# Output projection of a two-FFN transformer block: where its first loads stand, how many PSUM banks a chunk takes, and where its last six chunks stand

## The chip, the cores and the metric

The kernel runs on one core of a Trainium2 chip. A core has five engines with a queue of their own, each in order: TensorE (PE), VectorE (DVE), ScalarE (ACT), GpSimd (POOL) and SyncE (SP), which here only issues DMAs. They meet at semaphores. The metric is the device time of one execution in microseconds (us), as the median of several runs.

## The reference

The input x has 8 sequences of 1024 rows of 256 numbers, 8192 rows in all. Three residual steps follow each other:

```python
x = x + 0.5 * ffn(layernorm(x))     # gate/up 256 -> 704, SiLU, down 704 -> 256, every operand quantized to FP4 by blocks of 16
x = x + attn(layernorm(x))          # 16 heads of 16, causal softmax, then out @ Wo.T
x = x + 0.5 * ffn(layernorm(x))
```

The piece that matters here is the last product of the attention, `out @ Wo.T`, added to x, and the first rows of the second feed-forward.

## The kernel before, in words

The whole x stays in SBUF as `xs` (64 tiles of 128 rows). Four blocks follow each other, each ended by a barrier of all engines: feed-forward 0, the q/k/v projection, attention, and a last block in which the output projection stands ahead of feed-forward 1 (`feed_forward(1, store=True, begin=...)`). Within a block the order on each engine is the order in which its code is written; nothing is scheduled.

Attention works through 32 groups (8 sequences of 4 groups of 4 heads). A group's result is not yet divided by the softmax sums. SP carries it there: `send_half` writes the two halves (`o_all`) and their sums (`sum_rows`) to DRAM, `load_sums` brings the sums back and repacks the rows (`o_rows`), DVE takes the reciprocal (`one_over`), `load_group` sends it out (`inverse_rows`), spreads it over rows (`inverse_all`), and loads group and inverse, POOL multiplies (`divide`), and `send_out` stores into `attn_cols`, which holds the attention's output transposed, 256 x 8192. For the last group, the steps from `load_sums` on stand in the last block, among the output projection's own.

The output projection goes by 16 chunks of 512 rows. For chunk c: SP loads 256 x 512 numbers (512 KB) from `attn_cols` into one of four buffers (`out_a`, semaphore `a_loaded`); ACT rounds them to a high part (`out_aT_hi`), DVE takes the rest as the low part (`out_aT_lo`), both with two buffers; PE makes 24 matmuls (4 tiles of 128 rows, 2 halves of the contraction, 3 products of high and low parts) into two banks of PSUM; DVE adds the banks to `xs` (semaphore `resid`). A step of DVE is: low part of chunk c+1, then the sum of chunk c. PE's chunk c waits for `out_aT_lo` of c and for the sum of c-2; ACT's high part of c+1 waits for its load and for PE's chunk c-1.

`begin[name](eng, part)` stands ahead of the feed-forward's steps i = -6, -5 and -4 (`steps`). Part 0 holds chunks 0 to 11, part 1 chunks 12 and 13, part 2 chunks 14 and 15. Those feed-forward steps fill its pipeline: at step i DVE takes the layernorm's sums of tile i+6, ACT makes z of tile i+5 from POOL's `shift`, DVE reduces and quantizes z of tiles i+4 and i+3, PE transposes tile i+1 (`xT`), and the gate and up products of tile i come at step i (from step 0). In step i, DVE's `ffn_amax` of z leads to POOL's `ffn_dscale`, POOL's `ffn_shift` stands behind that, and ACT's next `ffn_z` waits for it.

Of the kernel before, what the change touches and what calls it, by code (L numbers as in the profile page):

```python
# [13 lines left out]
P = 128  # L14
# [12 lines left out]
CHUNK = 512  # L27
# [40 lines left out]
def build(nc, x_in, wq_in, wk_in, wv_in, wo_in, wg_in, wu_in, wd_in, y_out):  # L68
    V, S, G, T = nc.vector, nc.scalar, nc.gpsimd, nc.tensor
    top = ExitStack()  # L70
    with top:
# [41 lines left out]
        ring = [group_buffers(top, 0)]  # L113

# [222 lines left out]
        A_RING = 4  # L337
        a_loaded = [sem(f"a_loaded{i}") for i in range(A_RING)]

        def output_projection(ctx, last_group):  # L340

            s = out_sem
            CT = CHUNK // P
            CHUNKS = ROWS // CHUNK
            attn_in = sb(ctx, "out_a", [P, A_RING, KD, CHUNK], F32)
# [3 lines left out]
            def done(eng, name, c):  # L352
                if isinstance(c, int) and c < 0:
                    return
                eng.wait_ge(s[name], c + 1)

            def has(c):
                return not isinstance(c, int) or 0 <= c < CHUNKS

            def chunks(eng, step, part):  # L360

                if part == 0:
                    for c in range(-1, A_RING):
                        step(c, c % A_RING, c // A_RING)
                    with eng.Fori(1, CHUNKS // A_RING - 1) as turn:
                        for n in range(A_RING):
                            step(turn * A_RING + n, n, turn)
                for c in ((), (CHUNKS - 4, CHUNKS - 3), (CHUNKS - 2, CHUNKS - 1))[part]:
                    step(c, c % A_RING, c // A_RING)

            load_sums, load_group, send_out = last_group["sync"]

            def sync(sp, part):
                def step(c, r, turn):
                    if has(c):
                        done(sp, "aT_lo", c - A_RING)
                        sp.dma_start(attn_in[:, r, :, :], attn_cols[:, bass.ds(c * CHUNK, CHUNK)]
                                     .rearrange("(k p) c -> p k c", p=P)).then_inc(a_loaded[r], 16)
                    if isinstance(c, int) and c == A_RING - 1:
                        load_group(sp)  # L380

                if part == 0:
                    load_sums(sp)
                if part == 2:
                    send_out(sp)
                    sp.wait_ge(ao_stored, 32 * BATCH * GROUPS)
                chunks(sp, step, part)

            def tensor(pe, part):
                def step(c, r, turn):  # L390
                    if has(c):
                        done(pe, "resid", c - 2)
                        done(pe, "aT_lo", c)
                        for t in range(CT):
                            for k in range(KD):
                                for n, (x, w) in enumerate(passes(aT, woT)):
                                    last = T.matmul(proj_ps[r % 2][t // 2][:, (t % 2) * DIM:(t % 2 + 1) * DIM],  # L397
                                                    x[:, r % 2, k, t * P:(t + 1) * P], w[:, k, :],
                                                    start=k == 0 and n == 0, stop=k == KD - 1 and n == 2)
                        last.then_inc(s["proj"], 1)  # L400

                chunks(pe, step, part)
                if part == 2:
                    done(pe, "resid", CHUNKS - 1)

            def scalar(act, part):
                def step(c, r, turn):
                    if has(c + 1):
                        buf = (r + 1) % 2
                        nr, nturn = (r + 1) % A_RING, turn + (r + 1) // A_RING  # L410
                        act.wait_ge(a_loaded[nr], nturn * 16 + 16)
                        done(act, "proj", c - 1)
# [4 lines left out]
                chunks(act, step, part)  # L417
# [5 lines left out]
            def vector(dve, part):  # L423
                def step(c, r, turn):
                    if has(c + 1):
                        buf = (r + 1) % 2
                        done(dve, "aT_hi", c + 1)
                        for k in range(KD):
                            last = V.tensor_tensor(aT[1][:, buf, k, :], attn_in[:, (r + 1) % A_RING, k, :],  # L429
                                                   aT[0][:, buf, k, :].bitcast(F32), ALU.subtract)  # L430
                        last.then_inc(s["aT_lo"], 1)
                    if has(c):
                        done(dve, "proj", c)
                        for u in range(2):
                            rows = xs[:, bass.ds(c * CT + 2 * u, 2), :].rearrange("p t c -> p (t c)")
                            last = V.tensor_tensor(rows, proj_ps[r % 2][u][:, :], rows, ALU.add)  # L436
# [1157 lines left out]
```

## Time and profile before

| | |
|---|---|
| median of 3 runs | 2201.95 us (2199.97 to 2202.27) |
| profiled execution | 2202.19 us |
| its span in the trace | 2200.2 us, so 2.0 us lie around the span |
| attention's last value products on PE | until about 1660 |
| output projection on PE | 1671 to 1730 |
| first gate product of feed-forward 1 | 1740.46 |
| then to the end | about 6.8 us a tile |

The times in the trace are microseconds from the span's start. In the rows, a figure in brackets is the idle time of the engine ahead of an instruction, and what ended it. `SPq` is the queue of SP. PEclk is the granted clock of TensorE, 1.00 for 2.4 GHz and 0.50 for 1.2 GHz. A time for PE is one of pipelined matmuls, so neighbours overlap. An "x2" or "x24" is a run of like instructions merged into one row.

### The profile page before, as it was taken

To read this page: it belongs to the slowest core of one execution; us is meant where nothing else is said; L and a number is where in the kernel's file an instruction comes from. 1 tells how busy PE (TensorE), PEld (TensorE's weight loads), DVE (VectorE), ACT (ScalarE), POOL (GpSimd) and SP (SyncE) were. 2 spreads that over 40 slices of the span, in tenths; PEclk is the share of its full clock that TensorE was granted. 3 is DMA by queue.
4 is the path that set the end of the run, shared out by engine and by line. 5 is a ranking of instruction groups with operands and counts; after the bars stand their busy time and mean duration, and the time that the engine had idled before them with its cause. 6 is when DMAs were issued, how large, how long until landed. Compare 5 with 4: busy or idle time off the path is not lost. (4 is left out here: it accounts for less than half of the span.)

```text
span 2200.2 us, 44394 instructions
## 1 busy us (share of the span) xinstructions
PE 2041.9 (93%) x13448; PEld 1335.3 (61%) x13448; DVE 1906.2 (87%) x4327; ACT 1287.6 (59%) x2221; POOL 1037.8 (47%) x1639
## 2 busy tenths in 40 slices
PE   4799999997999799999999999999996799999998
PEld 3688888886885233333333333333335688888887
DVE  6799999996987789898888888898853699999996
ACT  3455555542763477777777777777783345555553
POOL 4788888883655011111111111111110388888884
PEclk9899999997997799999999999999998999999998
DMA  6000000001689477777777777877624100000000
GB/s 213 1 1 0 0 0 0 0 0 38 226 237 208 54 120 138 133 128 132 131 131 131 123 131 133 137 124 134 120 79 155 48 15 19 19 19 19 19 20 25
DMA packets 163502, 184.91 MB, mean 84 GB/s; under 512 B 57696, under 2 KB 109280, under 8 KB 163040
## 3 DMA queue, kind: packets, MB, share of 16 engines
q1 hardware_dynamic: 160672, 182.11, 39.6%
q8 instruction: 71, 1.16, 0.2%
q10 hardware_dynamic: 2688, 1.05, 0.2%
q14 instruction: 71, 0.58, 0.1%
HBM read 113.90 MB, written 85.98 MB: 91 GB/s over the span
## 5 line engine op out<-in xcount | busy, mean ns | idle before, releaser
L1476 POOL TENSOR_SCALAR_AFFINE_SELECT diag_scores<-diag_scores 128x256 f32<-128x256 f32 (+1 forms) x192 | 94.5, 493 | 581.4 <-ACT diag_scores L1439 577.5
L1512 DVE CUSTOM_DVE_ANT_0 gu_ps<-gu_ps,mask_qk 128x256 f32<-128x256 f32 x511 | 291.7, 597 | 73.7 <-PE gu_ps L1299 71.7
L1441 ACT ACTIVATE probs<-hT_ps 128x512 f32<-128x512 f32 (+3 forms) x320 | 273.7, 855 | 133.4 <-PE hT_ps L1321 75.9
L1299 PE MATMUL gu_ps<-k_stack,q_stack 96*128 96x512 bf16 (+3 forms) x994 | 319.2, 349 | 21.0 <-DVE part_max L1512 8.6
L721 PE MATMUL gu_ps<-wguT_hi,ffn_xT_hi 128*128 128x512 f32 (+1 forms) x768 | 313.1, 408 | 7.3 <-DVE ffn_xT_lo L597 5.1
L1340 PE MATMUL gu_ps<-probs,v_group 128*17 128x512 f32 (+3 forms) x3072 | 312.5, 494 | 2.2 <-ACT probs L1441 1.1
L721 PE MATMUL gu_ps<-wguT_hi,ffn_xT_lo 128*128 128x512 f32 (+1 forms) x768 | 290.2, 378 | 0.0
L721 PE MATMUL gu_ps<-wguT_lo,ffn_xT_hi 128*128 128x512 f32 (+1 forms) x768 | 289.8, 377 | 0.0
L699 ACT ACTIVATE ffn_z<-xs,ffn_shift,ffn_rstd 128x256 f32 (+1 forms) x128 | 77.1, 602 | 349.5 <-POOL ffn_shift L650 349.5
L1441 ACT ACTIVATE probs<-av_ps 128x512 f32<-128x512 f32 (+3 forms) x320 | 275.3, 860 | 0.6 <-PE av_ps L1321 0.5
L1299 PEld LDWEIGHTS gu_ps<-k_stack,q_stack 96*128 96x128 bf16 x994 | 91.8, 98 | 294.6 <-DVE part_max L1512 157.7
L1316 PE MATMUL hT_ps<-q_stack,k_stack 98*128 98x512 bf16 (+3 forms) x768 | 230.4, 330 | 8.6 <-DMA q_stack<-max_rows 8.2
L1517 DVE TENSOR_REDUCE part_max<-gu_ps 128x1 f32<-128x512 f32 x351 | 227.3, 678 | 10.3 <-PE gu_ps L1299 8.2
L620 POOL TENSOR_TENSOR ffn_hq<-ffn_g_h,ffn_nscale 128x704 f32<-128x704 f32 (+1 forms) x256 | 210.5, 843 | 3.5 <-DVE ffn_g_h L584 3.5
L752 PE MATMUL xd_ps<-wdT_hi,ffn_hT_hi 128*128 128x256 f32 x640 | 193.0, 302 | 20.5 <-DVE ffn_hT_lo L536 20.5
L1316 PE MATMUL av_ps<-q_stack,k_stack 98*128 98x512 bf16 (+3 forms) x768 | 193.4, 326 | 1.6 <-ACT probs L1441 1.3
L669 POOL TENSOR_TENSOR ffn_v_h<-ffn_h,ffn_rec 128x704 f32<-128x704 f32 x128 | 178.2, 1392 | 16.9 <-DVE ffn_rec L580 7.3
L752 PE MATMUL xd_ps<-wdT_lo,ffn_hT_hi 128*128 128x256 f32 x640 | 183.2, 286 | 0.0
L752 PE MATMUL xd_ps<-wdT_hi,ffn_hT_lo 128*128 128x256 f32 x640 | 183.2, 286 | 0.0
L1195 POOL TENSOR_TENSOR o_group<-o_group,o_inverse 128x512 f32<-128x512 f32 x32 | 40.7, 1272 | 267.4 <-DMA o_inverse<-inverse_all 267.4
L721 PEld LDWEIGHTS gu_ps<-wguT_hi,ffn_xT_hi 128*128 128x128 f32 x768 | 146.3, 191 | 26.8 <-DVE ffn_xT_lo L597 7.4
L721 PEld LDWEIGHTS gu_ps<-wguT_hi,ffn_xT_lo 128*128 128x128 f32 x768 | 145.5, 189 | 23.4
(211 smaller groups left out, 5120.0 us busy)
## 6 DMA issues: line engine op xcount, KB each, us to landing
q_stack<-q_parts SPq DMA_DIRECT2D x192, 128.0 KB, 7.0
k_stack<-k_parts SPq DMA_DIRECT2D x192, 128.0 KB, 7.6
o_all<-o_sb SPq DMA_DIRECT2D x64, 256.0 KB
q_parts<-qkv_parts SPq DMA_DIRECT2D x32, 384.0 KB, 2.7
k_parts<-qkv_parts SPq DMA_DIRECT2D x32, 384.0 KB, 2.8
v_ones<-qkv_vst SPq DMA_DIRECT2D x16, 544.0 KB, 3.8
v_group<-v_ones SPq DMA_DIRECT2D x32, 272.0 KB, 11.0
xs<-in_L_attn_x SPq DMA_DIRECT2D x8, 1024.0 KB, 12.0
```

Source lines behind the costliest of these rows:

```text
L620: last = G.tensor_tensor(blocks(hq[:, to:to + n]), blocks(g_h[:, of:of + n]), spread(nscale[:, par, of // BLK:(of + n) // BLK]), ALU.mult)
L669: G.tensor_tensor(blocks(v_h[:, par, :]), blocks(h[:]), spread(rec[:, OF_H]), ALU.mult).then_inc(s["v_h"], 1)
L699: S.activation(z[:, 1 - par, :], x_tile(i + 5), ACT.Identity, bias=shift[:], scale=rstd[:]).then_inc(s["z"], 1)
L721: last = T.matmul(gu_ps[:, n, 0:cols.stop - cols.start], x[:, buf, k * P:(k + 1) * P], w[:, k, cols], start=k == 0 and m == 0, stop=k == K ...
L752: T.matmul(down_ps, x[:, k * P:(k + 1) * P], w[:, k, :], start=k == 0 and n == 0, stop=False)
L1299: mm = T.matmul(out[:, e, :], qs[0:STACK, h0 + e, t * P:(t + 1) * P], ks[0:STACK, h0 + e, c * CHUNK:c * CHUNK + w], start=True, stop=True)
L1316: mm = T.matmul(scores[pair][:, e, at:at + w], ks[0:STACK_MAX, h, t * P:(t + 1) * P], qs[0:STACK_MAX, h, (j + 1) * CHUNK - w:(j + 1) * CHUNK],
L1340: mm = T.matmul(o_ps[h * VPAD:h * VPAD + VCOLS, CHUNK - w:CHUNK], vs[:, t, h, :], probs[:, h // 2, i % 2, h % 2, at:at + w], start=first, ...
L1441: S.activation(probs[:, pair, i % 2, :, first:w], scores[pair][:, :, first:w], ACT.Exp, scale=DH ** -0.5).then_inc(s[pr], 1)
L1476: G.affine_select(out=block_of, in_=block_of, compare_op=ALU.is_ge, fill=MASKED, base=0, pattern=[[0, 2], [0, count], [1, P]], channel_mul ...
L1512: last = V.tensor_tensor_reduce(out=ps[:, e * w:(e + 1) * w], in0=ps[:, e * w:(e + 1) * w], in1=mask_qk[:, CHUNK - w:CHUNK], scale=1.0, sc ...
L1517: last = V.tensor_reduce(part_max[:, h0:h0 + per, t, c], ps[:, 0:per * w].rearrange("p (h w) -> p h w", h=per), AX.X, ALU.max)
```

## The change

1. The buffers `out_a` are gone. The four chunk buffers are now the memory of the first group's `q_stack0` and `k_stack0` (two chunks each), which the last sequence's last three groups no longer use.
2. The loads of chunks 0 to 3 are issued by SP in the attention block, at its end: behind the last group's `load_inverse` (of the group before), ahead of its `send_half`.
3. `load_group` is cut in four steps, and in the last block they stand between loads: load 4, `send_inverse`, load 5, `spread_inverse`, load 6, `load_group`, load 7, `load_inverse`, load 8, 9, `send_out`, then the others.
4. A chunk's PSUM is `gu_ps` banks 0 and 1 for even chunks and the two banks of `hT_ps` for odd ones (before: `gu_ps` 0 and 1, `gu_ps` 2 and `xd_ps`). So ACT's copy, DVE's subtraction and DVE's sum are one instruction of 1024 columns a chunk each, where they were two of 512.
5. Part 0 holds chunks 0 to 9, and parts 1 to 6 one chunk each (10 to 15), ahead of the feed-forward's steps -5 to 0. `one_over` of the last group stands behind DVE's step 1 instead of step 0. All of it is unrolled, where chunks 4 to 11 were a loop.

```diff
+        attn_in = [ring[0][r // 2][:, :, :].bitcast(F32).rearrange("p h t -> p (h t)")[:, r % 2 * KD * CHUNK:(r % 2 + 1) * KD * CHUNK]
+                   .rearrange("p (k c) -> p k c", k=KD) for r in range(4)]
...
+        OUT_FIRST = 10
+        OUT_PARTS = OUT_CHUNKS - OUT_FIRST + 3
+        def load_out(sp, c):
+            out_done(sp, "aT_lo", c - A_RING)
+            sp.dma_start(attn_in[c % A_RING], attn_cols[:, c * CHUNK:(c + 1) * CHUNK]
+                         .rearrange("(k p) c -> p k c", p=P)).then_inc(a_loaded[c % A_RING], 16)
...
-            proj_ps = (bank[0:2], bank[2:4])
+            proj_ps = (gu_ps[:, 0:2, :], hT_ps[:, :, :])
+            def chunks(part):
                 if part == 0:
+                    return range(-1, OUT_FIRST)
+                return (OUT_FIRST - 1 + part,)
+
+            def sync(sp):
+                then = {A_RING: send_inverse, A_RING + 1: spread_inverse, A_RING + 2: load_group,
+                        A_RING + 3: load_inverse, A_RING + 5: send_out}
+                load_sums(sp)
+                for c in range(A_RING, OUT_CHUNKS):
+                    if c == SEQ // CHUNK * (BATCH - 1):
+                        sp.wait_ge(ao_stored, 32 * BATCH * GROUPS)
+                    load_out(sp, c)
+                    if c in then:
+                        then[c](sp)
...
+                if part == OUT_PARTS - 3:
+                    out_done(pe, "resid", OUT_CHUNKS - 2)
+                if part == OUT_PARTS - 1:
+                    out_done(pe, "resid", OUT_CHUNKS - 1)
...
-                        for k in range(KD):
-                            last = S.copy(aT[0][:, buf, k, :], attn_in[:, nr, k, :])
-                        last.then_inc(s["aT_hi"], 1)
+                        S.copy(aT[0][:, (c + 1) % 2, :, :], attn_in[(c + 1) % A_RING]).then_inc(s["aT_hi"], 1)
...
-                        if name in begin and i + AHEAD < 3:
+                        if name in begin and i + AHEAD < OUT_PARTS:
...
                         groups(sp, group)
+                        once(sp, "pv", (NG - GROUPS + 1) * NS, 0)
+                        for c in range(A_RING):
+                            load_out(sp, c)
                         send_half(*LAST, 1)
                         send_out(sp, *before(*LAST))
```

SP's queue at the seam of the two blocks, before. The names are a DMA's target and source; `out_a` are the chunk buffers.

```order
L1179 DMA o_inverse<-inverse_all 128x512 [waits att_inverse_spread]
L1239 DMA o_all<-o_sb 128x512 [waits att_o_sb]
L1240 DMA sum_rows<-o_sb 4x512
L1188 DMA attn_cols<-o_group 64x512 [waits att_ao]
L1188 DMA attn_cols<-o_group 64x512
L1232 UNCONDITIONAL_BRANCH
L770 UNCONDITIONAL_BRANCH [waits barrier_Pool_Activation_PE_DVE_SP_release]
L1159 DMA sums<-sum_rows 128x32 [waits att_inverse,att_o_sent]
L1161 DMA o_rows<-o_all 8x8192
L377 DMA out_a<-attn_cols 128x2x512 x4
L1168 DMA inverse_rows<-inverse 128x32 [waits att_inverse]
L1171 DMA inverse_all<-inverse_rows 128x1x512 [waits att_inverse_sent]
```

And with the change, from the first four loads on and from the new block's start on (the chunk buffers now read as `q_stack` and `k_stack`).

```order
L352 DMA q_stack<-attn_cols 128x2x512 [waits att_pv]
L352 DMA q_stack<-attn_cols 128x2x512
L352 DMA k_stack<-attn_cols 128x2x512 x2
L1229 DMA o_all<-o_sb 128x512 [waits att_o_sb]
```

```order
L1139 DMA o_rows<-o_all 8x8192
L352 DMA q_stack<-attn_cols 128x2x512 [waits out_aT_lo]
L1146 DMA inverse_rows<-inverse 128x32 [waits att_inverse]
L352 DMA q_stack<-attn_cols 128x2x512 [waits out_aT_lo]
L1153 DMA inverse_all<-inverse_rows 128x1x512 [waits att_inverse_sent]
L352 DMA k_stack<-attn_cols 128x2x512 [waits out_aT_lo]
L1162 DMA o_group<-o_rows 128x512 [waits att_o_packed,ao_stored]
L352 DMA k_stack<-attn_cols 128x2x512 [waits out_aT_lo]
L1169 DMA o_inverse<-inverse_all 128x512 [waits att_inverse_spread]
```

The first four loads moved ahead of the barrier and of `o_all`; loads 5 to 8 now stand each behind one of the steps that wait for the last group's inverse, where before all of them stood behind all those steps.

ACT's queue where the projection meets the feed-forward, before: the last two copies into `out_aT_hi` (two instructions each), and z, `av_ps` and `xT_hi` of the first tiles.

```order
L414 CAST out_aT_hi<-out_a 128x512 [waits out_proj,a_loaded2]
L414 CAST out_aT_hi<-out_a 128x512
L699 ACTIVATE ffn_z<-xs,ffn_shift,ffn_rstd 128x256 [waits ffn_shift,ffn_v_z]
L414 CAST out_aT_hi<-out_a 128x512 [waits out_proj,a_loaded3]
L414 CAST out_aT_hi<-out_a 128x512
L699 ACTIVATE ffn_z<-xs,ffn_shift,ffn_rstd 128x256 [waits ffn_shift,ffn_v_z]
L693 ACTIVATE av_ps<-ffn_v_z 128x256 [waits ffn_v_z,ffn_g_z,ffn_g_h]
```

With the change, chunks 11 to 15:

```order
L402 CAST out_aT_hi<-k_stack 128x1024 [waits out_proj,a_loaded3]
L678 ACTIVATE ffn_z<-xs,ffn_shift,ffn_rstd 128x256 [waits ffn_shift,ffn_v_z]
L402 CAST out_aT_hi<-q_stack 128x1024 [waits out_proj,a_loaded0]
L678 ACTIVATE ffn_z<-xs,ffn_shift,ffn_rstd 128x256 [waits ffn_shift,ffn_v_z]
L402 CAST out_aT_hi<-q_stack 128x1024 [waits out_proj,a_loaded1]
L672 ACTIVATE av_ps<-ffn_v_z 128x256 [waits ffn_v_z,ffn_g_z,ffn_g_h]
L678 ACTIVATE ffn_z<-xs,ffn_shift,ffn_rstd 128x256 [waits ffn_shift,ffn_v_z]
L402 CAST out_aT_hi<-k_stack 128x1024 [waits out_proj,a_loaded2]
L672 ACTIVATE av_ps<-ffn_v_z 128x256 [waits ffn_v_z,ffn_g_z,ffn_g_h]
L678 ACTIVATE ffn_z<-xs,ffn_shift,ffn_rstd 128x256 [waits ffn_shift,ffn_v_z]
L684 CAST ffn_xT_hi<-xd_ps 128x256 [waits ffn_xT,ffn_up]
L402 CAST out_aT_hi<-k_stack 128x1024 [waits out_proj,a_loaded3]
```

Each of the copies for chunks 12 to 15 now stands behind an `ffn_z` that waits for POOL's `ffn_shift`, and the last behind `ffn_xT_hi`, which waits for a transpose that PE makes behind chunk 14.

## Rows read from the trace of the kernel before

**Rows 1.** The page's head.
```profile
span 2200.2 us, 44394 instructions
```
**Rows 2.** Chain that ended last, in time: start, us, what.
```profile
1664.40 4.51 DMA out_a<-attn_cols
1668.94 1.15 ACT out_aT_hi L414 x2
...
1671.46 5.31 PE gu_ps L397 x24
...
1678.37 1.41 DMA inverse_rows<-inverse
1679.80 3.66 DMA inverse_all<-inverse_rows
...
1684.17 4.66 DMA out_a<-attn_cols
```
**Rows 3.** Timeline of SP's queue at the seam: start, us, engine, what.
```profile
1657.18 0.32 SPq L1179 DMA_DIRECT2D o_inverse<-inverse_all  x1
...
1661.45 1.16 SPq L1188 DMA_DIRECT2D attn_cols<-o_group  x2
1663.31 0.32 SPq L1159 DMA_DIRECT2D sums<-sum_rows  x1
...
1664.40 2.07 SPq L377 DMA_DIRECT2D out_a<-attn_cols  x4
```
**Rows 4.** Timeline of PE: chunk 4's first matmul, and one near the kernel's end.
```profile
1691.37 0.58 PE L397 MATMUL gu_ps<-woT_hi,out_aT_hi 128*128 128x256 f32 x1 [5.86 <-DVE out_aT_lo L429]
```
```profile
2181.00 0.36 PE L752 MATMUL xd_ps<-wdT_hi,ffn_hT_hi 128*128 128x256 f32 x1 [2.46 <-DVE ffn_hT_lo L536]
```
**Rows 5.** Stretches: us, busy PE, PEld, DVE, ACT, POOL, PEclk, DMA share, GB/s.
```profile
1662.70:1671.40 8.70, 0.00 (x0) 0.00 (x0) 1.29 (x2) 1.94 (x4) 0.00 (x0) 0.50 0.82 253
1740.40:1744.60 4.20, 4.14 (x11) 3.26 (x12) 1.89 (x8) 0.97 (x2) 3.02 (x8) 0.50 0.01 2
```
```profile
1671.40:1676.40 5.00, 4.94 (x23) 4.94 (x24) 1.30 (x3) 0.33 (x1) 0.00 (x0) 0.50 0.22 85
...
1691.30:1696.70 5.40, 5.33 (x25) 5.33 (x26) 2.41 (x5) 0.12 (x1) 0.00 (x0) 0.50 0.77 229
...
1711.40:1717.20 5.80, 5.80 (x49) 5.71 (x49) 4.98 (x8) 2.25 (x4) 0.00 (x0) 1.00 0.65 218
```
```profile
2181.00:2183.00 2.00, 2.00 (x11) 2.00 (x12) 0.89 (x1) 0.66 (x1) 1.38 (x2) 0.64 0.03 8
```
**Rows 6.** The same chain as in rows 2, from chunk 10's start to the feed-forward.
```profile
1711.33 4.39 PE gu_ps L397 x36
...
1718.61 0.44 DVE ffn_stats L540
...
1731.75 0.41 DVE ffn_amax L550
...
1733.06 0.61 ACT ffn_z L699
...
1739.50 0.36 ACT ffn_xT_hi L705
...
1740.46 2.93 PE gu_ps L721 x6
1743.39 0.43 PE xd_ps L737 x2
```
**Rows 7.** Timelines of DVE and POOL around the feed-forward's first step.
```profile
1719.17 1.26 DVE L429 TENSOR_TENSOR out_aT_lo<-out_a,out_aT_hi 128x512 fp32r<-128x512 f32 x2
1720.35 1.28 DVE L436 TENSOR_TENSOR xs<-gu_ps,xs 128x512 f32<-128x512 f32 x2
```
```profile
1719.33 0.55 POOL L632 TENSOR_TENSOR ffn_eps_var<-ffn_aggr,eps_tile 128x1 f32<-128x1 f32 x1 [31.66 <-DVE ffn_aggr L600]
...
1721.03 0.26 POOL L650 TENSOR_SCALAR ffn_shift<-ffn_aggr,ffn_rstd 128x1 f32<-128x1 f32 x1 [0.19 <-POOL ffn_rstd L635]
```

More of the change, by code:

```diff
@@ L346, in output_projection @@
             CT = CHUNK // P
-            CHUNKS = ROWS // CHUNK
-            attn_in = sb(ctx, "out_a", [P, A_RING, KD, CHUNK], F32)
             aT = [sb(ctx, f"out_aT_{part}", [P, 2, KD, CHUNK], F32R) for part in ("hi", "lo")]
-            proj_ps = (bank[0:2], bank[2:4])
[L352 to L358, printed above, removed]
@@ L360, in chunks @@
-            def chunks(eng, step, part):
-                if part == 0:
[L363 to L387, printed above, removed]
+            proj_ps = (gu_ps[:, 0:2, :], hT_ps[:, :, :])
@@ new lines, in output_projection @@
+            load_sums, send_inverse, spread_inverse, load_group, load_inverse, send_out = last_group["sync"]
+            def chunks(part):
+                if part == 0:
+                    return range(-1, OUT_FIRST)
[10 more added lines that the diff above has]
+                        then[c](sp)
@@ L389, in tensor @@
             def tensor(pe, part):
[L390 to L393, printed above, removed]
+                for c in chunks(part):
+                    if 0 <= c < OUT_CHUNKS:
+                        out_done(pe, "resid", c - 2)
+                        out_done(pe, "aT_lo", c)
                         for t in range(CT):
@@ L423, in vector @@
             def vector(dve, part):
[L424 to L436, printed above, removed]
-                        last.then_inc(s["resid"], 1)
-                    if isinstance(c, int) and c == 0:
+                for c in chunks(part):
+                    if c + 1 < OUT_CHUNKS:
+                        out_done(dve, "aT_hi", c + 1)
+                        V.tensor_tensor(aT[1][:, (c + 1) % 2, :, :], attn_in[(c + 1) % A_RING],
+                                        aT[0][:, (c + 1) % 2, :, :].bitcast(F32), ALU.subtract).then_inc(s["aT_lo"], 1)
+                    if 0 <= c < OUT_CHUNKS:
+                        out_done(dve, "proj", c)
+                        rows = xs[:, c * CT:(c + 1) * CT, :].rearrange("p t c -> p (t c)")
+                        V.tensor_tensor(rows, proj_ps[c % 2].rearrange("p a c -> p (a c)"), rows,
+                                        ALU.add).then_inc(s["resid"], 1)
+                    if c == 1:
                         last_group["vector"](dve)
-                chunks(dve, step, part)
-                done(dve, "resid", CHUNKS - 5 + 2 * part)
+                out_done(dve, "resid", 2 if part < OUT_PARTS - 1 else OUT_CHUNKS - 1)
             return {"sync": sync, "tensor": tensor, "scalar": scalar, "vector": vector, "gpsimd": gpsimd}
@@ L771, in _ @@
                         def _(sp):
-                            for part in range(3):
-                                if "sync" in begin:
-                                    begin["sync"](sp, part)
+                            if "sync" in begin:
+                                begin["sync"](sp)
                             with sp.Fori(0, TILES // 2) as it:
@@ L1162, in load_sums, with send_inverse @@
                              [:, 0:DH, :]).then_inc(s["o_packed"], 16)
-            def load_group(sp, b, g):
+            def send_inverse(sp, b, g):
                 n = b * GROUPS + g
@@ L1559, in _ @@
                         groups(dve, group)
-            return {"sync": (lambda sp: load_sums(sp, *LAST), lambda sp: load_group(sp, *LAST),
-                             lambda sp: send_out(sp, *LAST)),
+            return {"sync": [lambda sp, step=step: step(sp, *LAST) for step in
+                             (load_sums, send_inverse, spread_inverse, load_group, load_inverse, send_out)],
                     "vector": lambda dve: one_over(dve, *LAST), "gpsimd": lambda pool: divide(pool, *LAST)}
```

31 lines of the change are left out of this document (19 added, 12 removed).

## The prediction

> **What bounds the kernel now.** I read the page first, then the chain that ended last in order of time, then the timelines of SP, PE, DVE and POOL around the seam between attention and the last block, and last the table of stretches for TensorE's granted clock. The span is 2200.2 us [rows 1]. In the feed-forward the chain lies on PE tile after tile, so whatever lets the first gate product start sooner ends the kernel sooner by as much. That product starts at 1740.46 [rows 6]. The reader should look for what keeps it from starting earlier, and finds four things.
>
> First, the block's start. SP issues its last DMA of the attention block at 1661.45 for 1.16 us, and its first of the next block at 1663.31 [rows 3]: the barrier opens at about 1663.3. The first load of a chunk goes out at 1664.40 and takes 4.51 us; ACT's copy starts at 1668.94 and PE at 1671.46 [rows 2].
>
> Second, a hole behind chunk 3. The last group's inverse is sent at 1678.37, spread at 1679.80 in 3.66 us, and only then, at 1684.17, does SP issue load 4, which takes 4.66 us [rows 2]. PE is idle for 5.86 us ahead of 1691.37 [rows 4].
>
> Third, the clock. It is at 0.50 from 1662.7 on while PE idles, and stays there for chunk 0; it is there again for 5.40 us from 1691.3 (25 matmuls) and for 4.20 us from 1740.4 [rows 5]. At full clock 49 matmuls take 5.80 us [rows 5], so a chunk of 24 takes 2.85 us and two in a row have a pitch of about 2.9.
>
> Fourth, the seam with the feed-forward. From chunk 10's start at 1711.33 to the gate product 29.1 us pass [rows 6], for six chunks that need 17.4 at their pitch. The rest is a pipeline that fills through DVE, POOL and ACT with PE all but idle.
>
> **The change part by part.**
>
> Loads 0 to 3 in the attention block. SP is free at 1657.5, and four issues take 2.07 us [rows 3], so they are out by 1659.6, ahead of the wait for `o_sb` that held SP before. At 4.51 us [rows 2] the first lands at about 1662.1, before the barrier opens. From 1663.3, copy, low part and PE take what they took between 1668.94 and 1671.46, 2.5 us [rows 2]: PE starts at 1665.8 instead of 1671.46. Gain 5.65 us. Chunk 0 still runs at low clock, since PE idles here as well; I count no difference. Behind the four loads (2 MB) stand the last `o_all` and `sum_rows`, and `load_sums` waits for them. The first four loads kept the DMA engines busy until about 8 us after their first issue (DMA share 0.82 in the stretch to 1671.4 [rows 5]), so I put this wait's end near 1667, and load 4 at 1668.5, landing at 1673. ACT needs it when chunk 2 ends, at 1676.8: nothing, with 3.5 us to spare.
>
> Loads 4 to 8. Load 4 stands ahead of the inverse now, so the hole goes: 5.86 us, and the low clock behind it, 25 matmuls in 5.40 instead of 2.96, 2.4 us. Gain 8.3. What is late next is load 5. It stands behind `send_inverse`, which waits for `one_over`, now behind DVE's sum of chunk 1. Chunk 1 ends at about 1673.9 (5.2 at low clock, 2.9), its sum takes 1.28 [rows 7], so the inverse is there at 1675.5, load 5 goes out at 1675.9 and lands at 1680.6; ACT would take it at the end of chunk 3, 1679.7. Load 6 waits for the inverse's 1.41 us [rows 2] and shares the engines with the spread of 3.66 us: out at about 1678, landing near 1684, needed at 1683.5. Loads 7 and 8 come in time by the same count, by 1 to 2 us. I take 1.5 us for these waits; the bounds are 0 (all in time) and 5.9 (the old hole).
>
> Chunks 0 to 9 together: chunk 9 ends 12.4 us sooner than at 1711.33, at about 1698.9.
>
> Chunks 10 to 15 among the feed-forward's steps. Every engine keeps its order, so I follow the loop. From chunk 9's end: the sum of chunk 9 takes 1.28 [rows 7], the layernorm's statistics until POOL starts 0.72 (1718.61 to 1719.33 [rows 6, 7]), the low part of chunk 11 1.26 [rows 7]: PE starts chunk 11 at 3.3 instead of 2.9. POOL needs from 1719.33 to 1721.29 for its first three instructions [rows 7], `ffn_z` 0.61 [rows 6], then come the copy of chunk 12, 1.15 [rows 2], and its low part: 2.0 + 1.96 + 0.61 + 1.15 + 1.26 = 7.0. From here on one turn of the loop is: sum 1.28, statistics 0.44, from `ffn_amax` to the end of `ffn_z` 1.92 (1731.75 to 1733.67 [rows 6]), copy 1.15, low part 1.26, in all 6.05 us. Two turns bring chunk 14 to 19.1. PE takes 2.85 for it, then transposes, 0.43, ACT's `xT_hi` 0.36 [rows 6], the copy and low part of chunk 15, 2.4, and chunk 15, 2.85: 28.0, and with six handovers of 0.1 28.6. The gate product then follows at once, against 29.1 before. Gain 0.5: each turn costs the projection 3 us that it did not wait before, and hides as much of the filling.
>
> The cover is thin here. PE has 2.85 us of work in 6.05, so nothing on PE hides a slow turn; a tenth of a microsecond in the loop counts three times.
>
> The gate product at full clock. It comes straight behind chunk 15, not behind 7 us of near idleness. The 4.20 us at 0.50 [rows 5] go: gain 2.1.
>
> The clock in the new gaps. PE now idles for about 3.2 us ahead of chunks 13, 14 and 15. Rows 4 and 5 show that a gap of 2.46 us near the kernel's end was enough: the clock was at 0.64 over the 2 us behind it. A chunk at low clock takes 5.2 instead of 2.85. For chunk 13 this is hidden (it may end 2.9 us late), for 14 and 15 it is 2.35 each on the path. The bounds are 0 and 4.7, or 6.8 with the gate product; I take 1.5, since a slow chunk 13 fills its own gap.
>
> The Trainium skill says in "TensorE: Matmul & The Clock Gate", section "Loop structure matters more than you think", that matmuls spread out between long waits run cold, however the waits come about. It speaks against spreading the chunks; by it alone both chunks and the gate product would be slow, the term 6.8 and the time 5.3 us above mine.
>
> One instruction for two. Two neighbours of 512 columns take 1.26 to 1.28 us on DVE [rows 7]; one of 1024 does the same columns, and I count no gain. The extremes are nothing and one start, some 0.1 us, on each of the three instructions in a turn, 1 us in all; a loss I exclude, the same elements being read and written. The last load and the output's stores are far from any wait.
> The Trainium skill's "VectorE: DVE Perf Modes", section on the TRN2 errata, gives an f32 `tensor_tensor` of N columns (N+151)/0.96 ns, so 1.22 us for 1024, an estimate from that page. It would put 0.05 us per DVE pair on my sum's good side, some 0.4 us over the path.
>
> Sum: -5.65 - 8.3 + 1.5 - 0.5 - 2.1 + 1.5 = -13.5 us against this execution's 2202.19, so 2188.7 us. The median of the runs shown, 2201.95, stands 0.24 below the profiled one; I say 2188.5 us.
>
> **The rivals.**
>
> A. SP's order makes a new hole. For it: loads 5 to 8 each stand behind a step that waits for the same inverse as before, and my margins are 1 us or below. If every step slips by one landing under load (4.66 instead of the 3 or so left), the old 5.86 comes back nearly whole with its slow clock: 5.9 + 2.4 - 1.5 = 6.8 us worse, 2195.3. Against it: the inverse is asked for 3 us sooner, and one load is ahead of it.
>
> B. The clock falls in every gap, including the one before the gate product. 5.3 us worse, 2194. For it: rows 4 and 5 at the end of the kernel. Against it: chunk 15 leads straight into the gate product.
>
> C. All goes better: no wait at loads 5 and 6, no fall of the clock, and the single instructions save 1 us. 4 us better, 2184.5.
>
> D. Slower than before. The low clock takes hold at chunk 12 and lasts through the filling of the feed-forward, since that has gaps as well. Its price: 4.7 for chunks 14 and 15, 2.1 for the first tile, and 2.5 us for each further tile whose PE work is on the path; it decides from about four tiles on, 4.7 + 2.1 + 10 - 1.5 = 15.3, time 2204. Against it: the low stretches with dense work in rows 5 ended within 5.4 us of it.
>
> E. The early loads do not help: the barrier's opening or the last group's sums move out by as much, or PE's end of attention does not matter. At 5.65 us lost and load 4 late by some 5 more, 2199. Against it: they are issued before SP's wait for `o_sb` ends.
>
> **How the numbers follow.** My forecast, 2186 to 2191, gets 0.55; A 0.12; B 0.12; C 0.14; E 0.04; D 0.02; the 0.01 left is for something unseen on the same side as D. The range leaves out D, E and the outer halves of A and C: 2184.0 to 2194.5. A measurement of this kernel tells about 0.2% from no change, 4.4 us. Faster means below 2197.5: all but D, E and the rest, 0.94. Within 0.2%: E, with a part of D, 0.04. Slower: 0.02.
>
> **What would show it.** PE's first projection matmul 2.5 us behind the barrier and no DMA ahead of ACT's first copy shows the first step. No gap over 1.5 us ahead of chunk 4, and the largest ahead of chunk 5 or 6, released through a load, shows the second. Low parts of chunks 13, 14, 15 about 6 us apart, with ACT's copies released by `ffn_z` or `ffn_shift` and PE idle for 3 us, shows the loop. The gate product's first bank in 1.4 rather than 2.93 us shows the clock term. I am wrong if chunk 9 ends less than 10 us sooner, if the turns take over 7 us, or if the feed-forward takes longer from its first gate product on than before.

## The result, and the profile after

| | before | changed |
|---|---|---|
| median of 6 runs | 2199.44 us (2198.25 to 2202.27) | 2182.62 us (2178.45 to 2185.84) |
| profiled execution | 2202.19 us | 2184.42 us |

The ratio is 0.9921, 95% interval 0.9908 to 0.9934: 16.8 us between the medians, 17.8 between the profiled executions, where 13.5 were forecast. The time is below the stated range of 2184.0 to 2194.5. Part of that is the other kernel: the range was reckoned from a median before of 2201.95, and three more runs of that kernel brought it to 2199.44. As a gain the range is 7.5 to 18.0 us, and both measured gains lie in it, near its upper end.

The page's head, after [rows 1]:

```profile
span 2182.6 us, 44275 instructions
```

The chain that ended last, after: start, us, what [rows 2, 6].

```profile
1663.53 1.05 ACT out_aT_hi L402
...
1664.61 1.24 DVE out_aT_lo L412
...
1665.89 4.51 PE gu_ps L388 x24
...
1674.40 0.35 DVE inverse L1193
...
1674.77 1.41 DMA inverse_rows<-inverse
...
1676.92 5.69 DMA k_stack<-attn_cols
...
1682.63 1.06 ACT out_aT_hi L402
...
1720.81 4.35 PE hT_ps L388 x24
1725.16 1.39 PE gu_ps L700 x6
```

No load stands ahead of the first copy. PE starts 5.57 us sooner than at 1671.46, and the gate product (its first matmul is at 1724.99 in PE's timeline) 15.5 sooner than at 1740.46. Its first bank takes 1.39 us instead of 2.93.

The timeline of SP's queue at the seam, after [rows 3]:

```profile
1656.30 1.49 SPq L352 DMA_DIRECT2D q_stack<-attn_cols  x2
1657.83 1.32 SPq L352 DMA_DIRECT2D k_stack<-attn_cols  x2
1660.65 0.33 SPq L1229 DMA_DIRECT2D o_all<-o_sb  x1
...
1667.44 0.33 SPq L1137 DMA_DIRECT2D sums<-sum_rows  x1
...
1668.53 0.44 SPq L352 DMA_DIRECT2D q_stack<-attn_cols  x1
1674.77 0.33 SPq L1146 DMA_DIRECT2D inverse_rows<-inverse  x1
```

`load_sums` comes at 1667.44 (forecast near 1667), load 4 at 1668.53 (1668.5), the inverse at 1674.77 (1675.5).

PE's timeline, after [rows 4]: chunks 6, 13, 14, 15, and the first transposes of `h`.

```profile
1685.09 0.36 PE L388 MATMUL gu_ps<-woT_hi,out_aT_hi 128*128 128x256 f32 x1 [0.40 <-DVE out_aT_lo L412]
...
1709.22 0.35 PE L388 MATMUL hT_ps<-woT_hi,out_aT_hi 128*128 128x256 f32 x1 [2.43 <-DVE out_aT_lo L412]
1714.71 0.35 PE L388 MATMUL gu_ps<-woT_hi,out_aT_hi 128*128 128x256 f32 x1 [0.90 <-DVE out_aT_lo L412]
1720.81 0.55 PE L388 MATMUL hT_ps<-woT_hi,out_aT_hi 128*128 128x256 f32 x1 [2.81 <-DVE out_aT_lo L412]
...
1744.39 0.87 PE L742 MATMUL hT_ps<-ident,ffn_hq 128*128 128x128 f32 x3 [4.39 <-POOL ffn_hq L599]
```

The hole of 5.86 us ahead of chunk 4 is gone. The 0.40 ahead of chunk 6 is the largest gap on PE until chunk 12. The other gaps are those of the loop.

Stretches, after: us, busy PE, PEld, DVE, ACT, POOL, PEclk, DMA share, GB/s [rows 5].

```profile
1665.80:1670.40 4.60, 4.51 (x26) 4.51 (x27) 1.17 (x2) 0.00 (x0) 0.00 (x0) 0.65 0.55 178
...
1709.20:1712.10 2.90, 2.88 (x16) 2.90 (x17) 2.61 (x7) 0.33 (x1) 0.88 (x3) 0.64 0.02 6
...
1720.80:1725.10 4.30, 4.29 (x25) 4.30 (x26) 2.51 (x6) 0.60 (x1) 1.72 (x5) 0.67 0.00 0
1725.10:1728.20 3.10, 3.10 (x17) 2.52 (x16) 0.84 (x3) 0.37 (x1) 0.81 (x2) 1.00 0.00 0
```

The clock is low in a part of chunks 0, 13 and 15, and whole in the gate product.

DVE's timeline, after: the low parts of chunks 12, 13 and 14, whose distance is the turn of the loop, and one sum (answers to [rows 7]).

```profile
1702.36 1.22 DVE L412 TENSOR_TENSOR out_aT_lo<-q_stack,out_aT_hi 128x1024 fp32r<-128x1024 f32 x1 [1.08 <-ACT out_aT_hi L402]
1703.50 1.22 DVE L417 TENSOR_TENSOR xs<-hT_ps,xs 128x1024 f32<-128x1024 f32 x1
...
1707.85 1.23 DVE L412 TENSOR_TENSOR out_aT_lo<-q_stack,out_aT_hi 128x1024 fp32r<-128x1024 f32 x1 [1.38 <-ACT out_aT_hi L402]
...
1713.34 1.23 DVE L412 TENSOR_TENSOR out_aT_lo<-k_stack,out_aT_hi 128x1024 fp32r<-128x1024 f32 x1 [1.37 <-ACT out_aT_hi L402]
```

A turn is 5.49 us, not 6.05. ACT's timeline in one turn, after:

```profile
1706.28 0.60 ACT L678 ACTIVATE ffn_z<-xs,ffn_shift,ffn_rstd 128x256 f32<-128x256 f32 x1 [3.96 <-POOL ffn_shift L629]
1706.79 1.03 ACT L402 CAST out_aT_hi<-q_stack 128x1024 fp32r<-128x1024 f32 x1
```

ACT stands idle for 3.96 us ahead of `ffn_z`, which waits for POOL, and the copy, which waits for nothing else, comes behind it. The copy starts 0.51 us after a z of 0.60 us, as DVE's sum starts 1.14 after a low part of 1.22: neighbours overlap by 0.08 to 0.09 us.

### The profile page after: what moved, and what is told of

Its sections match the earlier page's. It is cut to its first block and busy times, and to the rows that moved or that the text cites. A ratio compares the mean times of both kernels' runs of the same rounds, so it can differ in the third digit from the quotient of the medians.

```text
span 2182.6 us, 44275 instructions
## 1 busy us (share of the span) xinstructions
PE 2033.3 (93%) x13448; PEld 1329.3 (61%) x13448; DVE 1904.7 (87%) x4295; ACT 1285.7 (59%) x2205; POOL 1039.5 (48%) x1639
```

## The experiments

The end of attention on PE differs between executions: its last value product ends at 1659.98 in the changed kernel's trace, at 1660.95 in a second trace of the same kernel (e8), and between 1655.5 and 1661.5 in all. So I compare traces from there. "PE" is the first projection matmul, "h" the first transposes of `ffn_hq` (1744.39 above). From "h" to the span's end it is 438.3 us before and 438.2 after (436.7 to 440.0 in the experiments). The next column starts at chunk 10's first matmul, so the front of the block is left out of it. Each trace is of one execution.

| | end of attention | to PE | to h | chunk 10 to h | median, us | ratio to before, 95% |
|---|---|---|---|---|---|---|
| before | 1659.83 | 11.63 | 102.04 | 50.70 | | |
| the change | 1659.98 | 5.91 | 84.41 | 47.92 | 2182.62 | 0.9921 [0.9908, 0.9934] |
| e1_late_loads | 1656.66 | 11.45 | 93.88 | 49.35 | 2191.63 | 0.9956 [0.9939, 0.9972] |
| e2_inverse_first | 1655.59 | 5.81 | 90.04 | 46.58 | 2184.95 | 0.9942 [0.9921, 0.9962] |
| e3_no_spread | 1657.19 | 5.81 | 86.41 | 49.34 | 2184.68 | 0.9935 [0.9913, 0.9957] |
| e4_halves | 1655.55 | 6.00 | 86.95 | 48.68 | 2186.00 | 0.9940 [0.9920, 0.9960] |
| e5_copy_ahead | 1660.42 | 5.88 | 80.26 | 43.29 | 2180.12 | 0.9899 [0.9882, 0.9917] |
| e6_warm | 1656.89 | 5.81 | 84.34 | 46.59 | 2183.39 | 0.9925 [0.9907, 0.9943] |
| e7_first12 | 1658.62 | 5.80 | 85.92 | 47.79 | 2183.30 | 0.9921 [0.9903, 0.9940] |
| e8_same | 1660.95 | 5.83 | 86.76 | 49.48 | 2183.01 | 0.9912 [0.9891, 0.9932] |
| e9_warm_start | 1660.04 | 6.05 | 83.59 | 48.02 | 2180.12 | 0.9910 [0.9894, 0.9926] |
| e10_ahead_warm | 1656.43 | 6.06 | 80.90 | 45.12 | 2176.14 | 0.9898 [0.9879, 0.9916] |
| e11_ahead_warm11 | 1661.50 | 6.07 | 77.67 | 42.25 | 2177.97 | 0.9899 [0.9881, 0.9916] |

Each ratio is to runs of the kernel before made together with the experiment's own; their medians are 2199.93 us for e1 to e4, 2201.31 for e5 to e8 and 2199.55 for e9 to e11. So medians of different sets are not to be compared to a microsecond.

How much one execution differs from the next shows in the column from chunk 10: e1, e2, e8 and e9 have the changed kernel's order from there on, and with the change's own trace they take 46.6 to 49.5 us. The two turns up to chunk 14 take 5.5 us each in all of them; what differs is where the clock is low.

### e1_late_loads: the first four loads back in the last block

```diff
-                        once(sp, "pv", (NG - GROUPS + 1) * NS, 0)
-                        for c in range(A_RING):
-                            load_out(sp, c)
...
-                for c in range(A_RING, OUT_CHUNKS):
+                for c in range(OUT_CHUNKS):
```

> Loads 0 to 3 go back behind the barrier and load_sums, all else stays as changed. Theory (each term stands by itself): ACT's first copy waits for the load again, PE's first projection matmul is 2.5 us behind that copy, at about 1671.4 instead of 1665.9, and all behind it moves by the same 5.6 us: the first gate product at about 1730.8, time about 12 us below before. Rival (the term is partly hidden, since the last sums come sooner when no 2 MB of loads stand ahead of them, and loads 5 to 8 then have slack): 4 us or less come back, time about 13.5 us or more below before.

It costs 9.5 us up to "h". ACT's timeline, for the copies of chunks 0 and 6:

```profile
1665.75 1.04 ACT L402 CAST out_aT_hi<-q_stack 128x1024 fp32r<-128x1024 f32 x1 [8.45 <-DMA q_stack<-attn_cols]
...
1686.77 1.05 ACT L402 CAST out_aT_hi<-k_stack 128x1024 fp32r<-128x1024 f32 x1 [3.36 <-DMA k_stack<-attn_cols]
```

The start is 5.5 of it (11.45 against 5.91), as reckoned. ACT stands 1.8 us ahead of the copies whose load is there; ahead of that of chunk 6 it stands 3.36, since later loads are late as well, and the waits for loads cost 1.5 more by chunk 9's end. Chunk 0 takes 5.49 us instead of 4.51, and chunk 15 is wholly at low clock, 5.46 instead of 4.35. Together 9.1. The first two, 7.0 us, follow from the edit. The last two also differ between executions of one kernel (e8), so I don't give them to it. The start came as expected, but the gate product is 74.13 us behind the end of attention against 65.01, 9.1 later and not 5.6, and the median is 8.3 us below its own before, where 12 were expected.

### e2_inverse_first: load 4 behind the last group's steps again

```diff
-                then = {A_RING: send_inverse, A_RING + 1: spread_inverse, A_RING + 2: load_group,
-                        A_RING + 3: load_inverse, A_RING + 5: send_out}
+                then = {A_RING + 5: send_out}
                 load_sums(sp)
+                for step in (send_inverse, spread_inverse, load_group, load_inverse):
+                    step(sp)
...
-                    if c == 1:
+                    if c == 0:
                         last_group["vector"](dve)
```

> All four steps of the last group's inverse stand ahead of load 4 again and one_over behind chunk 0, all else as changed. Theory (the hole behind chunk 3 and the low clock behind it are worth 8 us): the spread is out at about 1673.5, load 4 at 1678, PE idle for about 5.5 us ahead of chunk 4, low clock for it; the first gate product about 7 us later than with the change, time about 10 us below before. Rival (the early loads alone take the hole away, since all steps of the inverse move ahead with chunk 0): gap under 2 us, time within 2 us of the change's.

The chain in time, and PE's timeline at chunk 4:

```profile
1669.86 3.22 DMA inverse_all<-inverse_rows
...
1673.46 4.07 DMA q_stack<-attn_cols
...
1680.00 5.08 PE gu_ps L389 x24
1685.08 2.83 PE hT_ps L389 x24
```

```profile
1680.00 0.55 PE L389 MATMUL gu_ps<-woT_hi,out_aT_hi 128*128 128x256 f32 x1 [4.34 <-DVE out_aT_lo L413]
```

The hole is back with its slow clock: 4.34 for the gap and 5.08 - 2.83 = 2.25 for chunk 4. Chunk 9 ends 7.0 us later than in the changed kernel, counted from the end of attention. Of that, 0.75 less is waited at later loads, and 1.0 is chunk 0 (5.50 us here). By "h" 5.6 is left, since chunk 15 takes 2.96 here and 4.35 there. The second term stands by the rows. The median doesn't show it: it is 15.0 us below its own before, where 10 were expected, and its interval overlaps that of the change.

### e3_no_spread: chunks 12 to 15 in two parts, as before

PE's wait for the sum of chunk 14 ahead of part `OUT_PARTS - 3` goes with it.

```diff
-        OUT_PARTS = OUT_CHUNKS - OUT_FIRST + 3
+        OUT_PARTS = 3
...
-                    return range(-1, OUT_FIRST)
-                return (OUT_FIRST - 1 + part,)
+                return (range(-1, 12), (12, 13), (14, 15))[part]
```

> Chunks 10 and 11 back in part 0, 12 and 13 in part 1, 14 and 15 in part 2, all else as changed. Theory (the turns of the loop were over-counted, spreading is worth more than the 0.5 us of my sum): from chunk 9's end to the first gate product 29 us against 28.5 with the change, of which 1.5 were low clock, and the gate bank slow again for 2.1: 2.5 to 3.5 us above the change's time. Rival (spreading is worth nothing or costs, the whole gain is in the loads): within 1 us of the change or below it.

Stretches around the gate product, which starts at 1722.57:

```profile
1712.30:1722.50 10.20, 0.66 (x2) 0.29 (x2) 6.27 (x18) 3.12 (x7) 6.73 (x18) 0.67 0.00 1
1722.50:1726.00 3.50, 3.43 (x9) 2.75 (x10) 1.71 (x7) 0.60 (x1) 2.40 (x7) 0.51 0.00 0
```

PE is all but idle for 10 us, and the product then runs at 0.51. The product starts only 0.4 us later (65.38 from the end of attention, against 65.01), but "h" is 2.0 us later. From the gate product to "h" it takes 21.03 us against 19.40, so 1.6 of the 2.0 lie behind the product's start. That is below the 2.5 to 3.5 that were expected. Nor does it show that spreading gains: from chunk 10's start to "h" it is 49.34 here, 47.92 in the change's first trace and 49.48 in its second (e8). What the clean clock of the gate product gives, the low clock in chunks 13 to 15 can take back. The median can't tell 2 us either.

### e4_halves: two instructions of 512 columns, as before

```diff
-                        S.copy(aT[0][:, (c + 1) % 2, :, :], attn_in[(c + 1) % A_RING]).then_inc(s["aT_hi"], 1)
+                        for k in range(KD):
+                            last = S.copy(aT[0][:, (c + 1) % 2, k, :], attn_in[(c + 1) % A_RING][:, k, :])
+                        last.then_inc(s["aT_hi"], 1)
```

and the same for DVE's low part and its sum.

> Each copy, low part and sum is two instructions of 512 columns again, banks and order as changed. Theory (single instructions are a real part of what my sum lacked): each of the three costs 0.07 to 0.1 us more from start to start, the turn of the loop about 5.75 instead of 5.49 us, about 1.3 us later at the first gate product. Rival (the turn was short for another reason, the overlap of neighbours that I added up twice): turn 5.5, time within 0.4 us.

DVE's timeline, the low parts that answer to those of the changed kernel:

```profile
1699.62 1.29 DVE L415 TENSOR_TENSOR out_aT_lo<-q_stack,out_aT_hi 128x512 fp32r<-128x512 f32 x2 [0.85 <-ACT out_aT_hi L403]
...
1705.34 1.29 DVE L415 TENSOR_TENSOR out_aT_lo<-q_stack,out_aT_hi 128x512 fp32r<-128x512 f32 x2 [1.47 <-ACT out_aT_hi L403]
...
1711.06 1.29 DVE L415 TENSOR_TENSOR out_aT_lo<-k_stack,out_aT_hi 128x512 fp32r<-128x512 f32 x2 [1.46 <-ACT out_aT_hi L403]
```

A turn is 5.72 us, 0.23 more than with one instruction; the pitch in the dense part is 2.89 instead of 2.83. From the low part of chunk 11 to the gate product it is 27.35 us against 26.63. With nine pitches, merging gains 0.5 + 0.7 = 1.2 us, which I had put at nothing. Of the other 1.3 of the 2.5 at "h", 1.0 is chunk 0, 5.49 us here, and the rest is mostly a longer wait ahead of chunk 6. The turn of 5.72 is also the test of my 6.05, which was for these halves: 0.33 of the error was there without any merging.

### e5_copy_ahead: ACT's copy one part earlier

```diff
-                for c in chunks(part):
+                for c in (range(-1, OUT_FIRST + 1) if part == 0 else (OUT_FIRST + part,)):
```

> ACT makes each copy from chunk 12 on one part earlier, so that it stands ahead of the ffn_z that waits for POOL's shift (and chunk 15's copy ahead of xT_hi); all else as changed. Theory (the turn of 5.49 us is set by ACT's order: low part, sum, statistics, amax, POOL, z, copy, low part): copy and low part fall out of it, a turn is then z to amax to z through DVE's own work, about 4.3 us; the first gate product comes 4 us sooner than with the change, the gaps ahead of chunks 13 to 15 are under 1.7 us, no low clock there; time about 4 to 5 us below the change's. Rival (the turn is set by the feed-forward's own filling through POOL, the copy only sits in it): turn stays at 5 us or above, time within 1 us of the change's.

DVE's timeline of two low parts, and POOL's beside the first:

```profile
1706.63 1.57 DVE L412 TENSOR_TENSOR out_aT_lo<-q_stack,out_aT_hi 128x1024 fp32r<-128x1024 f32 x1
...
1711.02 1.57 DVE L412 TENSOR_TENSOR out_aT_lo<-k_stack,out_aT_hi 128x1024 fp32r<-128x1024 f32 x1
```

```profile
1706.51 0.62 POOL L635 TENSOR_TENSOR ffn_v_z<-ffn_z,ffn_rec 128x256 f32<-128x256 f32 x1
1707.21 1.13 POOL L642 TENSOR_SCALAR ffn_nscale<-ffn_amax 128x16 f32<-128x16 f32 x1
```

The low parts wait for nothing now, and a turn is 4.39 us: 1.1 less, and "h" comes 4.1 us sooner than with the change. So the turn is set by ACT's order, the copy behind an `ffn_z` that waits for POOL. Part of the 4.1 is the clock, which stays whole here from chunk 1 to "h", though the gaps ahead of chunks 13 and 15 are 1.82 and 2.36 us and not below 1.7 as expected. Against traces whose clock costs nothing from chunk 10 on (e2 and e6, 46.6 us to "h") the order alone gives 3.3. The median is 2.9 us below that of the changed kernel in the same set of runs (e8), where 4 to 5 were expected. The low parts now lie beside POOL's `ffn_v_z` and `ffn_nscale`; they take 1.57 us instead of 1.22, and `ffn_nscale` takes 1.13 where it takes 0.27 otherwise.

### e6_warm: matmuls in PE's gaps

Eight matmuls into a free bank, whose result nobody reads, ahead of the waits of chunks 13, 14 and 15.

```diff
+                        if 13 <= c <= 15:
+                            for _ in range(8):
+                                T.matmul(gu_ps[:, 2, :], wguT[0][:, 0, 0:P], wguT[0][:, 0, 0:CHUNK], start=True,
+                                         stop=True, skip_group_check=True)
```

> Eight extra matmuls of 512 columns (1.7 us) into the third bank of gu_ps, which nothing reads before the gate products overwrite it, stand ahead of each of chunks 13, 14 and 15; the outputs stay as they are. Theory (the low clock in chunk 15 comes from the gaps of 2.4 to 2.8 us and costs 1.4 us): no low clock between 1700 and 1725, chunk 15 in 2.85 us, the first gate product 1.4 us sooner. Rival (the clock falls for another reason, or the extra matmuls push the chunks back): low clock stays, or the gate product comes later by up to 1 us.

The stretch with all three gaps, and chunk 15:

```profile
1700.00:1722.00 22.00, 18.77 (x131) 16.61 (x131) 15.67 (x30) 6.79 (x12) 11.41 (x24) 1.00 0.04 16
1719.00:1722.00 3.00, 2.97 (x25) 3.00 (x26) 2.53 (x6) 0.42 (x1) 1.28 (x4) 1.00 0.00 0
```

The clock stays whole, and chunk 15 takes 2.96 us instead of 4.35. That alone would prove little, since e2 has 2.96 with the idle time left in. But e2's clock was low in chunk 13, and every one of the six traces that keep this loop's idle time (the change, e1, e2, e4, e8, e9) has it low in one or two of chunks 13 to 15. Of these seven only e6, where the idle time is filled, keeps it whole. So the idle time lowers it, as far as one trace against six can show. Up to "h" the gain is only 0.1 against the change's first trace, since the loop began 1.26 us later here (the low part of chunk 12 comes 43.64 after the end of attention, against 42.38: chunk 0 took 4.87 for 4.51, and the waits for loads were longer). From that low part to the gate product it is 21.30 against 22.63 us, 1.3 less, as expected. Against the second trace (e8) it is 2.4 up to "h". The median shows nothing.

### e7_first12: the spreading starts at chunk 12

```diff
-        OUT_FIRST = 10
+        OUT_FIRST = 12
```

> Twelve chunks in part 0 and one in each of parts 1 to 4. Theory (a chunk in a turn costs the projection 2.7 us more than in the dense part and hides as much of the filling, so where the spread starts moves little): the last chunk ends 5 to 6 us sooner than with the change, PE then waits 4 to 5 us for the first tile's z, the gate product comes 1 to 2 us sooner but at low clock again for its first bank; time within 1.5 us of the change's. Rival (each spread chunk is pure loss): 5 us below the change. Rival 2 (each is pure gain): 3 us above.

```profile
1722.50:1726.00 3.50, 3.44 (x9) 2.79 (x10) 1.65 (x6) 0.63 (x2) 2.38 (x8) 0.50 0.00 0
```

Counted from the end of attention, the projection ends 5.6 us sooner and the gate product comes 1.1 sooner, but at low clock again, as this stretch shows. "h" is within the change's own two traces, and from chunk 10 it takes 47.79 against 47.92: the place of the start hardly matters.

### e8_same: the changed kernel once more

> The changed kernel once more, unaltered. What differs here from its first trace is what one execution differs from the next: the end of attention's value products (at 1660.0 in its first trace), and where the clock falls. Theory: from that end to the first gate product 65 us within 1.5 us, by the clock alone. Rival: load times vary as well, the waits ahead of chunks 5 to 8 change by over 1 us.

The chain at chunk 15, and that stretch:

```profile
1722.61 5.46 PE hT_ps L388 x24
```

```profile
1722.60:1727.90 5.30, 5.29 (x25) 5.30 (x26) 2.51 (x6) 0.60 (x1) 1.73 (x5) 0.50 0.00 0
```

Same code, and the same gaps ahead of chunks 12 to 15 (0.97, 2.44, 0.93 and 2.82 us), but chunk 15 is wholly at low clock, and so is the start of the gate product. "h" is 2.35 us later: 1.1 for chunk 15, 0.4 for the gate product, 0.4 for a slower chunk 0 and 0.4 for waits at later loads. The gate product comes 66.9 us behind the end of attention, outside the 65 within 1.5 that I had expected, and not by the clock alone, though the waits changed by less than 1 us. A single trace tells differences under 2 us only where the rows show their cause.

### e9_warm_start, e10_ahead_warm, e11_ahead_warm11

e9 puts 11 unread matmuls behind attention's last value product and 11 at the start of the new block, to meet chunk 0 with a whole clock. e10 is e9 with e5's edit. e11 is e10 with `OUT_FIRST = 11`.

> The changed kernel with 11 extra matmuls of 512 columns (2.4 us) on PE right behind attention's last value products, and 11 more ahead of chunk 0, both into a bank of hT_ps that chunk 1 overwrites; outputs stay as they are. Theory (chunk 0 runs at low clock only because PE idles for 5.9 us ahead of it): chunk 0 in 2.9 instead of 4.5 to 5.2 us, all behind it 1.7 to 2.3 us sooner; time 2 us below the change's. Rival (the inverse's chain through SP then comes too late for loads 5 to 8, and takes it back): chunk 0 is short, but the waits ahead of chunks 5 and 6 grow by as much, time within 0.5 us of the change's.

> Both additions: the copies one part ahead and the matmuls that keep PE busy ahead of chunk 0. Theory (they stand by themselves): from the end of attention's value products to the first gate product 61 less 2, 59 us, against 65 with the change; time 6 to 7 us below the change's, near 2176. Rival: as with the rival of e9, 61 us and no less.

> As e10, with eleven chunks in part 0 instead of ten. Theory: the last chunk ends 1.4 us sooner, but the gate product then waits for the first tile's own filling by about as much; within 1 us of e10. Rival (a turn is still a loss of 1.5 us each to the projection): 1.5 us below e10.

Stretches: chunk 0 in e9, and the whole seam in e11.

```profile
1666.10:1668.90 2.80, 2.80 (x25) 2.80 (x24) 0.81 (x1) 0.00 (x0) 0.00 (x0) 1.00 0.36 102
```

```profile
1662.00:1740.00 78.00, 65.72 (x474) 60.44 (x473) 59.11 (x87) 28.82 (x40) 26.87 (x51) 1.00 0.37 122
```

Chunk 0 takes 2.83 us in e9 instead of 4.51. Of these 1.7 only 0.8 arrive at "h" against the first trace: in this execution the clock fell at chunk 14 instead (0.69 from 1712.0 to 1717.5), and 0.4 more is waited at later loads, so the rival came by about a quarter. In e10 the gate product comes 61.5 us behind the end of attention: the 61 of the rival, not the 59 expected. Chunk 0 is short there as well, but 0.65 more is waited ahead of chunk 6 than with the change, and the clock is low twice in the loop, for parts of chunks 13 and 15, behind gaps of 1.84 and 2.64 us:

```profile
1703.90:1707.40 3.50, 3.50 (x19) 3.50 (x19) 3.34 (x8) 0.60 (x1) 2.31 (x5) 0.51 0.02 5
1714.20:1717.60 3.40, 3.40 (x18) 3.40 (x18) 1.79 (x6) 0.60 (x1) 1.43 (x4) 0.50 0.00 0
```

In e11 it is whole all through, the gate product comes at 57.9, and "h" is 6.7 us sooner than with the change. That is 3.2 sooner than in e10. Against e5, whose clock is whole as well from chunk 1 on, it takes 42.25 us from chunk 10 to "h" instead of 43.29, so the place of the start is about 1 of it and the clock most of the rest. e10 and e11 have the lowest medians, 2176.14 and 2177.97. They beat the kernel before by some 1.0%. Their intervals still touch that of the change, which they lead by 4.7 to 6.5 us in the medians. e10's median is the 2176 expected; e11's is 1.8 above it, where within 1 was expected, against the order of their traces.

No run has the new PSUM banks, the later `one_over` or the unrolling changed alone, so what each is worth isn't shown.

## Why the prediction was wrong

The direction and the order of size were right, and so were the waits that were named, but the merged instructions were put at nothing and the turn of the loop was reckoned too long. The rivals A, B, D and E did not come. The sum was 4.3 us too small: against 2202.19 it gives 2188.7, and the profiled execution took 2184.42. The changed kernel's median lies another 1.8 below its profiled execution (I had put 0.2), as the median before came out 2.8 below its own. 4.0 of the 4.3 lie ahead of the gate product.

1. Start of PE: 1665.8 forecast, 1665.89 measured. e1 confirms its price, and shows 1.5 more of waits at later loads that the early loads save.
2. The hole: forecast 5.86 + 2.4, e2 gives 4.34 + 2.25 in a kernel that has the early loads. Right: the 5.86 and the slow chunk behind it are gone from the changed trace.
3. Chunk 0 at low clock: 5.2 forecast, 4.51 measured, 0.7 of the miss. Behind the same idle time it takes 4.5 to 5.5 us in other executions, so this part is luck.
4. Waits of loads 5 and 6: 1.5 forecast, 0.75 measured, 0.75 of the miss. The largest wait is the one named, for load 6, which takes 5.69 us in the chain; all of them together are half of what I took. The inverse was sent 0.7 us sooner than I put it.
5. Pitch of the dense chunks: 2.9 forecast, 2.83 measured, nine times, 0.6, of which 0.5 is the merging (e4). Chunk 9 ends at 1696.65 instead of 1698.9, by points 3, 4 and 5 and by 0.3 that my own pieces did not add up to, less 0.1 at the start.
6. The turn of the loop: 6.05 forecast, 5.49 measured, twice, 1.1. **This is the step that failed**, "one turn of the loop is: sum 1.28, statistics 0.44, ... in all 6.05 us", together with "one instruction for two ... I count no gain". 0.33 a turn is from adding up durations of neighbours that overlap (e4: 5.72 with the same halves), 0.23 from the merged instructions, which are worth 1.2 us over the whole path. The prediction itself says that a tenth in the loop counts three times. The six handovers of 0.1 overcount by another 0.6: from chunk 9's end to the low part of chunk 12 it is 5.71 us and from chunk 14's start to chunk 15's 6.10, where I had 5.72 and 6.04 without them. With the handovers this step is 1.7 of the 4.0, the largest part and still less than half; points 3 to 5 are the rest.
7. Gate product at full clock, gain 2.1: right. From its start to "h" it was 21.41 us before and is 19.40 after, 2.0 less. e3 shows the reverse, 1.6. In e8 the clock is low for the first of these matmuls, which costs 0.4, so the gain isn't had in every execution.
8. Low clock in the gaps: 1.5 forecast; chunk 15 took 4.35 instead of 2.85, so 1.5, and chunk 13's slow start filled its own gap ([0.90] ahead of chunk 14). The amount was met by chance: e8 has 2.6 in the same place, e2 0.1. The Trainium skill's "TensorE: Matmul & The Clock Gate", section "Loop structure matters more than you think", is borne out in kind (matmuls between waits lose the clock; e6 takes the waits' idle time away and keeps it), but not to the full 6.8 us. Its example of a loop that runs cold waits for a DMA each time, so the prediction's "however the waits come about" goes further than its words; here the waits are for DVE, and the clock fell as well.

The estimate of 1.22 us for one DVE instruction of 1024 columns is what the rows show (1.22), against 1.28 for two of 512. Two small slips changed nothing: the chances on the faster side add up to 0.93 and not 0.94, and the clock of chunk 4 before was still low at the end of the 5.40 us from which rival D took its 5.4. The price of spreading, -0.5 for the start, -2.1 and +1.5 for the clock, is not resolved by these runs (e3).

Rival C, "all goes better", is nearest to what came, yet for another reason than it gave: the clock did fall. Its 4 us were made of the waits (half of them came), the clock (nothing) and merging, whose bound of 1 us was below the 1.2 measured. The stated range ended 0.5 us below its 2184.5. It had no room for errors of adding up, which all lay on one side, nor for 2 us by which an execution's own clock moves the same kernel.

## What to carry to other kernels

To sum a loop that runs through several engines, take the distance between the starts of the same kind of row, where the trace has one, and not durations with a handover on each: on this chain that overcounted by 0.3 us in 6. Where spreading work over a pipeline's filling makes idle gaps on PE, look at what the last of them does to the first dense product, and at which engine's order sets the turn: a copy moved ahead of a waiting `ffn_z` gained 3.3 us beside the clock, the choice of the place 1 us at most (e7, e11). Price a merged instruction by its start, times the turns in which it is on the path.

## What the runs showed of the hardware that was not expected

- The granted clock is not a fixed answer to the same gap. The changed kernel's chunk 15, behind the same wait, took 4.35 us in one execution and 5.46 in another, and 2.96 in e2 with an unchanged loop.
- DVE's subtraction of 1024 columns takes 1.22 us alone and 1.57 beside POOL's work on SBUF in e5, and a POOL instruction of 16 columns takes 1.13 us instead of 0.27 beside it. In the changed kernel POOL's `ffn_eps_var`, of one column, takes 1.22 us beside the low part that starts at 1713.34, and 0.19 us a turn earlier.
- The next instruction on DVE starts 0.08 us before the one of 1.22 us ends by the records, and ACT's copy 0.09 before its z ends.
